# A decoder layer on one core: first operands in quarters, constant matmuls in the last block, and an earlier square-root table

## The reference

```python
rms = jnp.linalg.norm(query, axis=-1, keepdims=True) * e ** (-0.5)
x = query / (rms + EPS)
u = jax.nn.silu(jnp.einsum('nbe,fe->nbf', x, u_w) + u_b)
v = jax.nn.silu(jnp.einsum('nbe,fe->nbf', x, v_w) + v_b)
...                       # Toeplitz mix of v over tokens, u * y, output projection, layernorm
...                       # cross attention with 16 heads, layernorm
h = jax.nn.silu(jnp.einsum('btd,efd->btef', x, W1))      # 8 experts, the best 2 of each token
y = jnp.einsum('btef,edf->bted', h, W2)
out = jnp.einsum('bte,bted->btd', gate, y)
x = _layernorm(x + out, axis=-1)
```

## Time and profile before

| | before |
|---|---|
| median of 3 runs | 643.27 us (642.83 to 643.72) |
| profiled execution | 643.63 us, of which 642.0 us are the span of the trace |
| PE busy | 621.9 us, 97% of the span |
| DVE busy | 442.4 us, 69% |
| ACT busy | 340.1 us, 53% |
| PE's longest idle times | 3.9 us at 295, 3.0 us at 5, 2.2 us at the start |

### The profile page before, as it was taken

One profiled execution on the slowest core, in us unless ns is written; L12 is line 12 of the kernel. 1 busy time (PEld: TensorE's weight loads), 2 busy tenths in 40 slices (PEclk: granted clock), 3 DMA queues, 4 the chain that ended last, 5 costly groups with the idle time before them and its releaser, 6 DMA issues.

```text
span 642.0 us, 9647 instructions
## 1 busy us (share of the span) xinstructions
PE 621.9 (97%) x3802; PEld 533.5 (83%) x3802; DVE 442.4 (69%) x606; ACT 340.1 (53%) x436; POOL 146.2 (23%) x136
## 2 busy tenths in 40 slices
PE   6999999999989999997999999999999999999996
PEld 5799978879978888796888888888878889888984
DVE  3565636545269995758786676776776759798985
ACT  4843532115335565634664564656555669566745
POOL 2150000001557885004610000000000000183531
PEclk9999999999999999968999999999999999999995
DMA  8993006004700003202985656566556668898412
GB/s 309 401 381 132 2 20 275 1 0 160 284 1 1 3 1 114 85 2 89 318 291 170 231 215 214 200 234 222 193 216 214 234 211 299 287 339 316 152 48 102
DMA packets 26374, 111.81 MB, mean 174 GB/s; under 512 B 3848, under 2 KB 4872, under 8 KB 16730
## 3 DMA queue, kind: packets, MB, share of 16 engines
q1 hardware_dynamic: 21108, 97.00, 41.9%
q0 software_dynamic: 3536, 11.11, 5.0%
q10 hardware_dynamic: 1686, 3.10, 1.4%
HBM read 92.17 MB, written 19.03 MB: 173 GB/s over the span
## 4 chain that ended last, share of the span: by engine, by line
PE 85%; DVE 9%; ACT 2%; issue 2%; DMA 1%; POOL 0%; SPq 0%; ACTq 0%
PE bank L1978 16%; PE bank L1644 15%; PE bank L1646 15%; PE bank L1645 15%; PE bank L1970 8%; PE bank L1679 2%; PE bank L1701 2%; PE bank L2127 2%; PE bank L2022 2%; DVE probs L1183 2%; DVE row_sum L1195 1%; DVE row_max L1189 1%; PE bank L1864 1%; DMA raw<-in_pieces 1%; PE bank L1921 1%
## 5 line engine op out<-in xcount | busy, mean ns | idle before, releaser
L1978 PE MATMUL bank<-xg_cat,whi 128*128 128x480 f32 (+3 forms) x512 | 155.0, 367 | 3.9 <-DVE xg_cat L1389 3.9
L1382 DVE TENSOR_TENSOR wlo<-raw,whi 128x2048 fp32r<-128x2048 f32 x54 | 123.0, 2289 | 28.8 <-ACT whi L912 28.6
L1970 PE MATMUL bank<-xg_cat,wlo 128*128 128x240 f32 (+3 forms) x512 | 114.0, 263 | 0.0
L912 ACT ACTIVATE whi<-raw 128x2048 fp32r<-128x2048 f32 x54 | 102.0, 1908 | 21.1 <-PE bank L1646 14.2
L1970 PEld LDWEIGHTS bank<-xg_cat,wlo 128*128 128x128 f32 x512 | 95.5, 191 | 5.4
L1978 PEld LDWEIGHTS bank<-xg_cat,whi 128*128 128x128 f32 x512 | 89.8, 190 | 10.4 <-DVE xg_cat L1389 4.1
L1644 PE MATMUL bank<-whi,h_cat 128*120 128x512 f32 (+2 forms) x208 | 82.5, 397 | 0.0
L1646 PE MATMUL bank<-whi,h_cat 128*120 128x512 f32 (+2 forms) x208 | 82.1, 395 | 0.0
L1645 PE MATMUL bank<-wlo,h_cat 128*120 128x512 f32 (+2 forms) x208 | 82.0, 394 | 0.0
L876 ACT ACTIVATE hidden<-hidden 128x480 f32<-128x480 f32 (+3 forms) x64 | 34.8, 553 | 70.9 <-DVE hidden L1398 70.0
L1398 DVE TENSOR_TENSOR hidden<-bank,cross 128x480 f32<-128x480 f32 (+3 forms) x64 | 37.0, 587 | 31.8 <-ACT cross L869 31.8
(11 more groups left out here) (282 smaller groups left out, 1284.6 us busy)
## 6 DMA issues: line engine op xcount, KB each, us to landing
raw<-in_ffn_pieces SPq DMA_DIRECT2D x64, 1024.0 KB, 5.3
raw<-in_pieces SPq DMA_DIRECT2D x11, 1024.0 KB, 11.0
routed<-zeros SPq DMA_DIRECT2D x27, 256.0 KB, 5.4
expert_out<-zeros SPq DMA_DIRECT2D x15, 256.0 KB
xg<-routed POOLq DMA_DIRECT2D x8, 240.0 KB, 5.4
expert_out<-y_sb ACTq DMA_DIRECT2D x8, 240.0 KB
x<-in_x_tok SPq DMA_DIRECT2D x1, 1536.0 KB, 11.3
out<-x SPq DMA_DIRECT2D x6, 256.0 KB, 2.0
```

Source lines behind the costliest of these rows:

```text
L912: act.activation(whi[slot][:], raw[slot][:], ACT.Copy)\
L1382: dve.tensor_tensor(wlo[slot][:], raw[slot][:], f(whi[slot][:]), ALU.subtract)\
L1970: pe.matmul(o[:, 0:c], w_l[:, k, ft * P:(ft + 1) * P], xg_cat[:, k, 0, 0:c], start=False, stop=False)
L1978: mm = pe.matmul(o.rearrange("p (x c) -> p x c", x=2), w_h[:, k, ft * P:(ft + 1) * P], xg_cat[:, k, :, 0:c], start=(k == 0), stop=(k == KD ...
```

## The change

The operands of the first product come in quarters: one feature block of the input and one of V0 at a time, and each quarter gets all three of its products (with it the last 400 tokens of `x_feat` come in two parts, and the last 32 rows of tokens are sent for ahead of the whole tiles). Three more constant matmuls stand ahead of it. Two `u_scale` stand ahead of the making of `mix`, one behind it and ahead of `split_lo(V1)`. In the last block four constant matmuls stand ahead of the transposes of the last feature block, and three ahead of the wait for the last `final_hi`. ACT takes a square root of a constant behind the last silu, whose result nobody reads.

```diff
-WARM = 5
+WARM = 8
+WARM_TURNED = 4
+WARM_SPLIT = 3
...
-    X_PARTS = [(slice(0, 2), slice(0, HT)), (slice(2, KD), slice(0, HT)), (slice(0, KD), slice(HT, T))]
+    X_PARTS = [(slice(k, k + 1), slice(0, HT)) for k in range(KD)]
+    X_PARTS += [(slice(0, KD), slice(HT, 5 * P)), (slice(0, KD), slice(5 * P, T))]
+    V0_PART = [slice(512 * k, 512 * (k + 1)) for k in range(KD)]
...
-            load_x(0)
-            sp.dma_start(raw[0][:, 0:1024], pieces[V0][:, 0:1024]).then_inc(v0_in, 16)
-            load_x(1)
-            sp.dma_start(raw[0][:, 1024:2048], pieces[V0][:, 1024:2048]).then_inc(w_in[0], 16)
-            load_x(2)
+            for k in range(KD):
+                load_x(k)
+                sp.dma_start(raw[0][:, V0_PART[k]], pieces[V0][:, V0_PART[k]]).then_inc(v0_in[k] if k < KD - 1 else w_in[0], 16)
+            load_x(KD)
+            load_x(KD + 1)
+            sp.dma_start(x[0:LAST, FULL, :], x_tok[FULL * P:T]).then_inc(x_in, 16)
             sp.dma_start(x[:, 0:FULL, :], x_tok[0:FULL * P].rearrange("(t p) d -> p t d", p=P)).then_inc(x_in, 16)
-            sp.dma_start(x[0:LAST, FULL, :], x_tok[FULL * P:T]).then_inc(x_in, 16)
...
-            x_hi(0)
-            act.wait_ge(v0_in, 16)
-            act.activation(whi[0][:, 0:1024], raw[0][:, 0:1024], ACT.Copy).then_inc(v0_hi, 1)
...
+            for k in range(KD):
+                x_hi(k)
+                act.wait_ge(v0_in[k] if k < KD - 1 else w_in[0], 16)
+                act.activation(whi[0][:, V0_PART[k]], raw[0][:, V0_PART[k]], ACT.Copy).then_inc(v0_hi if k < KD - 1 else w_hi, 1)
+            x_hi(KD)
+            x_hi(KD + 1)
...
+            act.activation(std3_col[:, 0:1], eps_col[:], ACT.Sqrt)
             act.wait_ge(h_sum[1], 8 * len(LATE))
...
             split_lo(U1)
-            split_lo(V1)
+            dve.wait_ge(scale_row_done, 2)
+            u_scale(0, 0)
+            u_scale(0, 1)
...
-            dve.wait_ge(scale_row_done, 2)
-            for n in range(8):
+            u_scale(0, 2)
+            split_lo(V1)
+            for n in range(3, 8):
                 u_scale(0, n)
...
+            for k in range(KD):
+                pe.wait_ge(xf_hi_done, k + 1)
+                pe.wait_ge(*((v0_hi, k + 1) if k < KD - 1 else (w_hi, 1)))
                 for t in range(EARLY):
...
+                    pe.matmul(bank[:, 4 + t, :], xf_hi[:, k, t * P:(t + 1) * P], w_hi0[:, k, :], start=(k == 0), stop=False)
+                pe.wait_ge(xf_lo_done, k + 1)
                 for t in range(EARLY):
...
+                    pe.matmul(bank[:, 4 + t, :], xf_lo[:, k, t * P:(t + 1) * P], w_hi0[:, k, :], start=False, stop=False)
+                pe.wait_ge(*((v0_lo, k + 1) if k < KD - 1 else (w_lo, V0 + 1)))
+                for t in range(EARLY):
                     mm = pe.matmul(bank[:, 4 + t, :], xf_hi[:, k, t * P:(t + 1) * P], w_lo0[:, k, :],
                                    start=False, stop=(k == KD - 1))
...
             for t in range(EARLY, TILES):
+                pe.wait_ge(xf_lo_done, KD + 1 if t < 5 else KD + 2)
                 v_tile(0, t)
...
                     pe.wait_ge(final_split, j - 1)
+                if j == KD - 1:
+                    keep_warm(4, WARM_TURNED)
                 pe.wait_ge(yt_done, j + 1)
...
             pe.wait_ge(yt_done, KD)
+            keep_warm(7, WARM_SPLIT)
             pe.wait_ge(final_read, KD)
```

More of the change, by code:

```diff
@@ L290, in decoder_layer @@
     x_in, small_in, o_bias_in, bias2_in = sem("x_in"), sem("small_in"), sem("o_bias_in"), sem("bias2_in")
-    xt_in = [sem(f"xt_in{c}") for c in range(3)]
-    v0_in, v0_hi, v0_lo = sem("v0_in"), sem("v0_hi"), sem("v0_lo")
+    xt_in = [sem(f"xt_in{c}") for c in range(KD + 2)]
+    v0_in = [sem(f"v0_in{k}") for k in range(KD - 1)]
+    v0_hi, v0_lo = sem("v0_hi"), sem("v0_lo")
     consts = sem("consts")
@@ L697, in gated_hi @@
                    .then_inc(y_hi, 1)
-            x_hi(0)
-            act.wait_ge(v0_in, 16)
-            act.activation(whi[0][:, 0:1024], raw[0][:, 0:1024], ACT.Copy).then_inc(v0_hi, 1)
-            x_hi(1)
-            act.wait_ge(w_in[0], 16)
-            act.activation(whi[0][:, 1024:2048], raw[0][:, 1024:2048], ACT.Copy).then_inc(w_hi, 1)
-            x_hi(2)
+            for k in range(KD):
[4 more added lines that the diff above has]
+            x_hi(KD + 1)
             act.wait_ge(consts, 15)
@@ L1072, in gate @@
                 dve.tensor_tensor(lo[:, j, :], u_feat[:, j, :], f(hi[:, j, :]), ALU.subtract).then_inc(y_lo, 1)
-            x_lo(0)
-            x_lo(1)
-            dve.wait_ge(v0_hi, 1)
-            dve.tensor_tensor(wlo[0][:, 0:1024], raw[0][:, 0:1024], f(whi[0][:, 0:1024]), ALU.subtract)\
-               .then_inc(v0_lo, 1)
-            dve.wait_ge(w_hi, 1)
-            dve.tensor_tensor(wlo[0][:, 1024:2048], raw[0][:, 1024:2048], f(whi[0][:, 1024:2048]), ALU.subtract)\
-               .then_inc(w_lo, 1)
-            x_lo(2)
+            for k in range(KD):
+                x_lo(k)
+                dve.wait_ge(*((v0_hi, k + 1) if k < KD - 1 else (w_hi, 1)))
+                dve.tensor_tensor(wlo[0][:, V0_PART[k]], raw[0][:, V0_PART[k]], f(whi[0][:, V0_PART[k]]), ALU.subtract)\
+                   .then_inc(v0_lo if k < KD - 1 else w_lo, 1)
+            x_lo(KD)
+            x_lo(KD + 1)
             dve.wait_ge(rms_done, 1)
@@ L1706, in _ @@
             EARLY = HT // P
-            for kh, hi_ready in ((0, v0_hi), (1, w_hi)):
-                ks = range(2 * kh, 2 * kh + 2)
-                pe.wait_ge(xf_hi_done, kh + 1)
-                pe.wait_ge(hi_ready, 1)
+            for k in range(KD):
+                pe.wait_ge(xf_hi_done, k + 1)
+                pe.wait_ge(*((v0_hi, k + 1) if k < KD - 1 else (w_hi, 1)))
                 for t in range(EARLY):
-                    for k in ks:
-                        pe.matmul(bank[:, 4 + t, :], xf_hi[:, k, t * P:(t + 1) * P], w_hi0[:, k, :],
-                                  start=(k == 0), stop=False)
-                pe.wait_ge(xf_lo_done, kh + 1)
+                    pe.matmul(bank[:, 4 + t, :], xf_hi[:, k, t * P:(t + 1) * P], w_hi0[:, k, :], start=(k == 0), stop=False)
+                pe.wait_ge(xf_lo_done, k + 1)
                 for t in range(EARLY):
-                    for k in ks:
-                        pe.matmul(bank[:, 4 + t, :], xf_lo[:, k, t * P:(t + 1) * P], w_hi0[:, k, :],
-                                  start=False, stop=False)
-            pe.wait_ge(v0_lo, 1)
-            pe.wait_ge(w_lo, V0 + 1)
-            for t in range(EARLY):
-                for k in range(KD):
+                    pe.matmul(bank[:, 4 + t, :], xf_lo[:, k, t * P:(t + 1) * P], w_hi0[:, k, :], start=False, stop=False)
+                pe.wait_ge(*((v0_lo, k + 1) if k < KD - 1 else (w_lo, V0 + 1)))
+                for t in range(EARLY):
                     mm = pe.matmul(bank[:, 4 + t, :], xf_hi[:, k, t * P:(t + 1) * P], w_lo0[:, k, :],
                                    start=False, stop=(k == KD - 1))
-                mm.then_inc(v_mm, 1)
-            pe.wait_ge(xf_lo_done, 3)
+                    if k == KD - 1:
+                        mm.then_inc(v_mm, 1)
             for t in range(EARLY, TILES):
+                pe.wait_ge(xf_lo_done, KD + 1 if t < 5 else KD + 2)
                 v_tile(0, t)
```

## The result

| | median us | runs | ratio to before, 95% |
|---|---|---|---|
| before | 643.05 | 641.14 to 643.72 (4) | |
| with the change | 635.71 | 633.27 to 637.03 (4) | 0.9899 [0.9867, 0.9931] |
| before, beside the last experiments | 643.25 | 638.73 to 644.13 (11) | |
| with the change, beside them | 636.06 | 632.31 to 637.51 (6) | 0.9884 [0.9848, 0.9921] |

The account below looks back on a forecast made before the run. PE was taken as the bound (85% of the chain that ended last), idle or slow at both ends. 643.63 - 3.65 (head) - 2.5 (end) = 637.5, 637.1 against the median; forecast 637.3, range 635.8 to 640.2.

Parts of the forecast that it names:

- The first operands: Head: with operands in quarters, PE's first V0 product starts at 6.2, 1.45 us earlier than 7.67.
- the lower level: Head: V0's products lose 0.4 us to the lower clock level (1.2 GHz), from bounds of 0 and 2.0.
- U0's low part: Head: tokens 0.4 us earlier, U0 ready at about 27.0; PE starts on it at 27.2, 3.05 us earlier.
- The second rival: Head: ten transfers in SP's queue delay the tokens, U0 ready at 29.2, head gains 1.65 us: 639.1; chance 0.11.
- the third rival: Head: short transfer rows cost as much as long, tokens 3.9 us late: 640.8; slower by over 0.2%: chance 0.03.
- The scalings: Head: two scalings moved ahead remove PE's wait before the fifth `u_half`, ending at 39.98: 0.6 us.
- The head together: Whole head: 3.65 us gained, bounds 1.9 and 4.2; `mix_head` at 45.2, not 48.82.
- The middle: From `mix_head` to 619: order unchanged, the head's gain carried whole, 0.5 us allowed each way for the clock.
- The end: Last block: constants hold the clock at 1.00, DVE becomes the bound; 2.5 us gained, bounds 0.4 loss, 3.2 gain.
- The first rival: Last block: the clock falls at the end all the same, tail loses 0.4 us: 640.0; chance 0.13.
- The table: Last block: the 1.28 us load costs nothing behind ACT's last silu; left in place, some 0.9 us at full clock.

Follow-up runs that it names:

- the head's and the end's own: Head only: the changed kernel without its last-block constants and early table, 640.58 us. End only: the kernel before plus those two, 640.11 us.

## Why the prediction was right or wrong

The forecast was 637.3 us with a range of 635.8 to 640.2, and the chance of faster 0.95. The kernel is faster; its medians are 635.71 and 636.06, so the forecast was 1.2 to 1.6 us too high, which is hardly more than a measurement can tell; the second lies in the range and the first 0.1 us under its foot. That the sum came so near is in part luck: the head gave 1.0 to 1.4 us less than predicted, the end 0.9 more, and the middle about 1.5 that no term had.

- **The first operands.** PE was to enter at 6.2 and entered at 5.73: eight constants took 3.5 us, not 4.0. V0 was to end at 26.1 and ended at 26.56, since the lower level and one wait (0.31) cost 1.3 us more than the products themselves, where 0.4 was taken from bounds of 0 and 2.0. That cost differs among executions: in the eleven profiles in which the input comes in as with the change it is 0.3 to 1.6 us. The first three products alone take 1.62 us here and 0.93 in six others. The spreading was well priced at 1.05, going by the distance between starts (25.95 to 26.99 with the tokens in three parts). So PE could have begun U0 at about 27.6, where 27.15 was predicted.
- **U0's low part, the step that failed.** "I take 0.4, so U0 is ready at about 27.0": it was ready at 28.91. The tokens were to come 0 to 0.9 us earlier, and ACT's first square came 1.6 us later (0.5 to 1.9 in the six profiles with this head). PE began U0 at 28.97 and not 27.2. The second rival had nearly these numbers: the first square at 17.9 and U0 ready at 29.2, and it was 17.59 and 28.91. Whether it also had the mechanism, the ten transfers' time in SP's queue, is not shown. SP was past the ten at about 6, as the argument against it said, and past the last 32 rows at 7.22; the whole tiles landed 10.24 us behind that. What the rows show is that the bytes ahead went slower: from 2.20 to 7.70 the DMA engines moved 243 GB/s and not 313, at a share of 0.88 and not 0.95. That is 385 KB less, 1.2 us at 313 GB/s (an estimate from these rows), and since the share fell far less than the rate, most of it is not the engines standing and waiting for SP. Shorter rows, the third rival's mechanism at a part of its 3.9 us, would look like that, and so would a cost of each transfer; no run here separates them. The tokens in three parts show the price of the wait for U0's low part, 1.2 us.
- **The scalings.** The mechanism was right, two of them ahead of the mix matrix, no wait before the fifth `u_half`, and the term in the sum was small but fair: from U0's first product to `mix_head` it was 18.57 us before and 17.58 after, 1.0 us less where 0.6 was taken. What the edit is worth beside the others was missed: 6.2 us, because without it the earlier PE and the later tokens would have met in a wait of 3.3 us, with half the clock behind it. The right question was what the wait would be without the move, not what it was.
- **The head together:** 3.65 us were predicted, 2.3 measured in the profile (2.6 over the six profiles with this head, mean 46.2), and 4.1 with the tokens in three parts.
- **The middle.** "I carry the head's gain whole", with 0.5 us each way. The head's gain was carried whole, but the allowance was far too small. The middle alone gave 3.5 us in the one profile, 1.6 in the other and 0 in the head's and the end's own. Three runs within 0.9 us had looked like a narrow spread; 62 show three groups over 6 us. The medians seem to contain about 1.5 us of it: by the stages 643.2 - 2.6 - 3.3 = 637.3 would be the change's own effect (an estimate), and 635.7 and 636.1 were measured.
- **The end.** 2.5 us were predicted, 3.4 measured, a little over the bound of 3.2. The delay by the constants was to be 0.4 and was 0. The seventh addition was to come 6.65 us behind the first and came 6.08 behind it: the two written tiles ahead of it cost 0.46 each and not 0.55, and the inversions hide. And the bound is not quite DVE, as the text said, but ACT at 1.03 us a tile: the chain's last 7 us run through its squares and roots, and DVE waits 0.29 us for the last root.
- **The first rival** (the clock falls all the same) didn't come in any of the eleven profiles with the constants, nor in a run that the mean clock can tell. **The third** (every row costs the same) didn't come at its price; the tokens were 1.6 us late, not 3.9.
- **The table** cost nothing in its new place, and would have cost 1.2 us (0.9 predicted) in the old one. The drain that the Trainium skill adds was rightly left out.

## What to carry to other kernels

When one engine is made earlier, look at the next thing that it will wait for at its new time and move that too: here three moved lines decided between a gain of 2.6 us and a loss of 3.6. A single large transfer that a chain waits for can land in parts, each with its own count: here that took 1.2 us of PE's wait out of the profiled head, though the medians are too coarse to show it. And where the granted clock dips in thin work, take many executions before and after: the dip comes and goes by itself, a profile of one execution tells what the clock did in it and not what the edit did, and constant matmuls in the waits are worth their time where they turn a frequent fall into none, as at the end here; in the router stage the number that costs no more than the fall was not found.

## What was not expected of the hardware

- The same kernel, with its instructions in the rows ahead within 0.01 us of each other, had a granted clock of 1.00 from 276 to 284 us in one execution and 0.50 in another, at a cost of about 2 to 3.5 us. Of the runs with waits of 0.67 and 0.56 us behind dense work 46 of 84 lie at the low mean clock that goes with a fall at the end beside the router stage's.
- A wait of 3.32 us on PE was followed by 6 us at the lower level, and so cost 6.2 us in all.
- With ten transfers of 200 to 480 KB queued where five of 400 to 800 KB had been, the DMA engines moved 243 GB/s from 2.20 to 7.70 us at a share of 0.88, as the row in the part on the head shows, and 313 at 0.95 before.
